# First stage of a layer kernel: order of root, exponentials and softmax weights, order in the last group, and earlier loads of the first patches

## The chip, the cores and the metric

One core of one Trainium2 chip runs the kernel. The metric is device time in microseconds, from one launch to its end. Clock figures are the granted TensorE clock in the profile, as a share of 2.4 GHz.

## The reference

Two images of 256 channels and 96x96 pixels pass one layer: a convolutional part whose nine filter taps per pixel are themselves computed and put through a softmax, and a mixture of experts (two of eight). Cut to what matters here:

```python
def _branch(x, w, d):
    f = lax.conv_general_dilated(x, w, (1, 1), [(d, d), (d, d)], rhs_dilation=(d, d), ...)   # 9 taps per pixel
    f = jax.nn.softmax(f.reshape(N, g, K, H * W), axis=2)
    patches = jnp.stack([xp[:, :, i * d:i * d + H, j * d:j * d + W] for i in range(3) for j in range(3)], axis=2)
    return jnp.einsum('ngrkp,ngkp->ngrp', patches, f)

outs = [x]                                   # x is the layer-normed input here
for w, d in zip((w_a, w_b, w_c, w_d), (1, 4, 8, 12)):
    outs.append(_branch(x, w, d))
y = conv1x1(concatenate(outs), w_proj) + b_proj
x = x + relu(group_norm(y))
x = x + moe(layer_norm(x))                   # router, top 2 of 8 experts, gelu, gated sum
```

## The kernel before

The program runs in stages that all engines leave and enter together (`leave`, `enter`). Each image has a first stage (layer norm, the tap products and the softmax weights) and a second one (the patches are multiplied by their weights and projected); then come the router, the experts and the sum. The change lies in the first stage and at the start of the second.

**First stage.** `GROUPS` = 24 steps `k`, each for `R` = 4 rows of the image. Every engine runs its own written-out list of instructions, in order, and they meet by semaphores. In step `k`:

- TensorE: `channels(k)` turns the normalised rows `xn` back into channels (`ps_ch`); `late_products(k-1)` makes taps 2 and 3 and the two own products of the group before; `tap_products(k, 0)`; `tokens(k+2)` transposes the input of the group after next (L831); `tap_products(k, 1)`. All products go to the two banks of `ps_a` in turn: product `n` waits until product `n-2` has been kept (`wait_free`; the order stands in the list `units`).
- ScalarE: `xc_hi` (L1276), `normalise(k+1, (0, 1))` (`xn`, L1232, needs `nmr`), then copies the late products out (`g_rows` L1241, `y_acc` L1249), `normalise(k+1, (2, 3))`, `keep_products(k, 0)`, in some steps `exponentials`, then `deviation(k+2)` (square root, `std`, L1225) and `keep_products(k, 1)`.
- VectorE: `xc_lo` (L1620), the high half of `rows_st` (L1624), in some steps `lower` (logits less their maximum, L1589 to L1594), `statistics(k+2)` (L1568, L1571), the low half of `rows_st` (L1630), `factors(k+2)` (`rstd`, `nmr`, L1576, L1578), in some steps `weights` (L1602 to L1615).
- GpSimd adds the tap products of the group to the running sums `taps` (L2141).
- SP loads `x_in` and stores `rows_st` to `rows_scratch` in DRAM.

Three groups give a batch of 12 rows; there are 8. Batch `b` is summed up (`logits`, 16 matmuls, L875) in step 3b+7, exponentiated and weighed in that same step, and its filters are turned (`turn_filters`, 2x6 transposes, L885) in step 3b+8. Batches 6 and 7 come behind the last group: their logits wait until GpSimd has added group 23 (`taps_added`). `f_pow` holds one batch's exponentials, `f_low` two batches' logits, later weights; `f16` holds one batch in half precision, and `weights(b)` waits for the turned filters of batch b-1 before it writes it.

**Second stage.** 64 steps. The first 16 are strips, each with 8 loads of patches (112 KB each) from `rows_scratch`: 6 are issued by SP (L677), 2 by GpSimd (L2183), into a ring of three buffers `patches`. The first buffer lies where `x_in` and part of `xn` lie in the first stage. TensorE computes `band(0, 0)`, `band(0, 1)`, `band(1, 0)` (L929), then the branches `ps_o` (L992), which need the patches, and the projections `ps_y`.

## Time and profile before

| | us |
|---|---|
| timed runs, median (lowest to highest) | 2487.01 (2482.56 to 2492.95) |
| profiled execution | 2486.36 |
| its span | 2484.5 |
| first stage, image 0 and image 1 | 21 to 304, 704 to 975 |
| second stage, image 0 and image 1 | 304 to 704, 975 to 1460 |
| mean granted TensorE clock | 0.876 |

| engine | busy us | share of the span |
|---|---|---|
| TensorE | 1950.0 | 78% |
| VectorE | 1626.7 | 65% |
| ScalarE | 1274.9 | 51% |
| GpSimd | 1058.6 | 43% |

The shares are means over stages with different limits, so they say little of one stage. To read the first stage, take the chain of waits: the path of work back from the last instruction, each piece with its start and its length. Then take the same microseconds engine by engine: an entry in square brackets at the end of a line is the idle time in front of the instruction and who ended it. A line that groups several instructions (x8) shows the first start and the time from there to the end of the last. PE is TensorE, DVE VectorE, ACT ScalarE, POOL GpSimd.

### The profile page before, as it was taken

To read this page: it belongs to the slowest core of one execution; us is meant where nothing else is said; L and a number is where in the kernel's file an instruction comes from. 1 tells how busy PE (TensorE), PEld (TensorE's weight loads), DVE (VectorE), ACT (ScalarE), POOL (GpSimd) and SP (SyncE) were. 2 spreads that over 40 slices of the span, in tenths; PEclk is the share of its full clock that TensorE was granted. 3 is DMA by queue.
4 is the path that set the end of the run, shared out by engine and by line. 5 is a ranking of instruction groups with operands and counts; after the bars stand their busy time and mean duration, and the time that the engine had idled before them with its cause. 6 is when DMAs were issued, how large, how long until landed. Compare 5 with 4: busy or idle time off the path is not lost.

```text
span 2484.5 us, 60548 instructions
## 1 busy us (share of the span) xinstructions
PE 1950.0 (78%) x20124; PEld 1843.4 (74%) x20125; DVE 1626.7 (65%) x4385; ACT 1274.9 (51%) x2717; POOL 1058.6 (43%) x1444
## 2 busy tenths in 40 slices
PE   4788699999968886999999928723999999993322
PEld 4677599999957775999999927723999999992222
DVE  3465465656555654777887848852788899894653
ACT  4566343333336663556666626512777777771211
POOL 2454412323225543146566614775555555551000
PEclk9999799999989997999999966556999999995555
DMA  5222155566632222677898787743666444446897
GB/s 135 82 77 77 50 177 149 139 173 169 167 107 83 77 64 86 194 208 241 254 269 263 232 277 250 249 162 128 197 207 192 155 159 162 153 157 212 294 302 252
DMA packets 334948, 433.66 MB, mean 175 GB/s; under 512 B 87469, under 2 KB 260141, under 8 KB 333805
## 3 DMA queue, kind: packets, MB, share of 16 engines
q1 hardware_dynamic: 260945, 294.85, 40.3%
q0 software_dynamic: 41024, 97.10, 11.1%
q10 hardware_dynamic: 32784, 39.07, 4.7%
q8 instruction: 128, 2.10, 0.4%
q14 instruction: 67, 0.55, 0.1%
HBM read 277.12 MB, written 159.94 MB: 176 GB/s over the span
## 4 chain that ended last, share of the span: by engine, by line
PE 47%; DMA 16%; DVE 12%; issue 9%; POOL 6%; ACT 6%; SPq 2%; DVEq 2%; POOLq 0%; ACTq 0%
PE ps_y L418 15%; PE ps L418 9%; DMA expert_out<-e_out,dest 6%; PE ps_a L418 6%; PE ps_o L992 6%; POOL expert_in L2204 5%; PE ps_b L929 4%; DMA o_acc<-res_scratch 3%; DMA o_y<-expert_out 3%; DVE stats L1568 2%; PE ps_x L1140 1%; PE ps_tok L831 1%; PE ps_a L875 1%; DVE rows_st L1630 1%; DVE cat_lo L1663 1%
## 5 line engine op out<-in xcount | busy, mean ns | idle before, releaser
L418 PE MATMUL ps_y<-cat_hi,wp 128*128 128x288 f32 x2048 | 473.7, 307 | 1.9 <-DVE cat_lo L1663 1.9
L2227 POOL DMA_INDIRECT expert_out<-e_out,dest x304 | 306.8, 1009 | 233.2 <-DMA expert_out<-e_out,dest 94.4
L2183 POOL DMA_DIRECT2D patches<-rows_scratch x352 | 196.8, 601 | 468.2 <-PE ps_o L979 262.4
L2141 POOL TENSOR_TENSOR taps<-taps,g_rows 96x108 f32<-96x108 f32 (+3 forms) x440 | 236.9, 566 | 271.5 <-ACT g_rows L1241 267.7
L418 PEld LDWEIGHTS ps_y<-cat_hi,wp 128*128 128x128 f32 x2048 | 346.4, 190 | 2.1 <-issue 1.1
L418 PE MATMUL ps_y<-cat_lo,wp 128*128 128x288 f32 x1024 | 303.8, 297 | 0.0
L1309 ACT ACTIVATE bands<-ps_b 112x288 f16<-112x288 f32 (+4 forms) x256 | 105.3, 411 | 342.9 <-PE ps_b L929 333.0
L1663 DVE SCALAR_TENSOR_TENSOR cat_lo<-ps_o,cat_hi 128x288 fp32r<-128x288 f32 (+1 forms) x576 | 227.3, 419 | 63.9 <-ACT cat_hi L1315 59.5
L1315 ACT ACTIVATE cat_hi<-ps_o 128x288 fp32r<-128x288 f32 (+1 forms) x576 | 212.9, 384 | 65.1 <-PE ps_o L979 30.6
L418 PE MATMUL ps<-e_hi,w_now 128*128 128x256 f32 x1216 | 242.6, 282 | 0.6 <-issue 0.2
L1655 DVE SCALAR_TENSOR_TENSOR bands<-ps_b,bands 112x288 f16<-112x288 f32 (+4 forms) x256 | 116.6, 455 | 191.4 <-ACT bands L1309 188.6
L418 PE MATMUL ps<-w,h_hi 128*128 x1216 | 234.4, 291 | 3.6 <-DVE h_lo L2043 3.6
L992 PE MATMUL ps_o<-bands,patches 112*128 112x72 f16 (+2 forms) x4608 | 193.1, 199 | 24.7 <-DVE cat_lo L1663 14.0
L418 PE MATMUL ps_a<-wg,xc_hi 128*96 128x324 f32 x768 | 187.0, 329 | 29.0 <-ACT g_rows L1241 19.1
L1194 PE MATMUL ps_t<-ident,o_sum 128*128 128x128 f32 x288 | 73.8, 429 | 163.1 <-DVE o_sum L2099 163.1
L2204 POOL DMA_INDIRECT expert_in<-c_ln,pos x144 | 150.5, 1045 | 117.3 <-DVE pos L1899 70.5
L418 PEld LDWEIGHTS ps<-e_hi,w_now 128*128 128x128 f32 x1216 | 197.6, 189 | 3.0 <-issue 2.1
L418 PEld LDWEIGHTS ps_y<-cat_lo,wp 128*128 128x128 f32 x1024 | 195.6, 191 | 0.0
L992 PEld LDWEIGHTS ps_o<-bands,patches 112*128 112x128 f16 (+2 forms) x4608 | 172.0, 101 | 31.6 <-issue 30.4
L1485 ACT ACTIVATE e_act<-ps,b_now 128x256 f32<-128x256 f32 x304 | 127.9, 472 | 121.3 <-PE ps L418 115.7
L1194 PEld LDWEIGHTS ps_t<-ident,o_sum 128*128 128x128 f32 x288 | 54.8, 221 | 181.9 <-issue 172.0
L418 PEld LDWEIGHTS ps<-w,h_hi 128*128 128x128 f32 x1216 | 185.5, 189 | 4.6 <-issue 4.4
(241 smaller groups left out, 4939.1 us busy)
## 6 DMA issues: line engine op xcount, KB each, us to landing
e_x<-expert_in SPq DMA_DIRECT2D x152, 260.0 KB
o_y<-expert_out SPq DMA_DIRECT2D x48, 768.0 KB, 5.3
patches<-rows_scratch SPq DMA_DIRECT2D x160, 192.0 KB
patches<-rows_scratch SPq DMA_DIRECT2D x256, 108.0 KB
patches<-rows_scratch SPq DMA_DIRECT2D x192, 112.0 KB
x_in<-in_x SPq DMA_DIRECT2D x48, 384.0 KB, 3.2
rows_scratch<-rows_st SPq DMA_DIRECT2D x48, 384.0 KB, 3.0
y_scratch<-y_acc SPq DMA_DIRECT2D x48, 384.0 KB
```

The costliest lines, as they stand in the source:

```text
L418: mm = eng.matmul(out, lhs[p], rhs[q], start=start and n == 0, stop=stop and n == 2)
L992: mm = pe.matmul(out, ring[:, (2 * p + z) * C + c * 128:(2 * p + z) * C + (c + 1) * 128], band_of[:, q, p * 72:(p + 1) * 72], start=k == 0 ...
L1194: mm = pe.transpose(ps_t[:, u, c, k * 128:(k + 1) * 128], o_sum[:, u, k, c * 128:(c + 1) * 128], ident[:])
L1309: act.activation(bands[0:k, s % 2, 0, first:first + n], ps_b[0:k, 0:n], ACT.Relu).then_inc(band_hi_done, 1)
L1315: act.activation(cat_pixels(cat_hi[:, s % 2, c], s, j), out_pixels(ps_o[:, n % 2], s), ACT.Copy, scale=UNSCALE).then_inc(cat_hi_done, 1)
L1485: last = act.activation(e_act[:, u, f], ps_1[:, u, f], ACT.Gelu, bias=b1_now[:, u, f:f + 1])
L1655: dve.scalar_tensor_tensor(out=bands[0:k, s % 2, 1, first:first + n], in0=ps_b[0:k, 0:n], scalar=0.0, in1=bands[0:k, s % 2, 0, first:first ...
L1663: dve.scalar_tensor_tensor(out=cat_pixels(cat_lo[:, s % 2, c], s, j), in0=out_pixels(ps_o[:, n % 2], s), scalar=UNSCALE, in1=cat_pixels(ca ...
L2141: last = pool.tensor_tensor(here, here, g_rows[:, u, first:end, i, b:b + nb].rearrange("p r b k -> p r (b k)"), ALU.add)
L2183: pool.dma_start(patch_target(s, n), patch_source(m, s, n)).then_inc(patch_pooled[s % RING], 16)
L2204: pool.indirect_dma_start(out=xs_dram, out_offset=bass.IndirectOffsetOnAxis(ap=at, axis=0), in_=c_ln[:, v, k // TT, k % TT], in_offset=Non ...
L2227: pool.indirect_dma_start(out=ys_dram, out_offset=bass.IndirectOffsetOnAxis(ap=at, axis=0), in_=e_out[:, u, j], in_offset=None).then_inc(e ...
```

## The change

- **Square root**: `deviation(k+2)` moves behind `keep_products(k, 1)` on ScalarE.
- **Exponentials**: both of a pair of batches run in the step of the odd batch (steps 10, 16, 22), in place in `f_low`; `f_pow` goes, and the wait for `f_dve` with it.
- **Weights** (VectorE): batch b (even) one step behind its pair's exponentials, b+1 two steps behind; they stand between `statistics(k+2)` and the low half of `rows_st`. The filters are turned one step after that, so the second one's in the step in which the next pair's first logits come. Batch 4 is weighed in step 23, batch 5 behind the steps.
- **Last group**: taps 2 and 3 first, then the own products with the turned filters of batch 4 between them, the turned filters of batch 5, then the logits of 6 and 7 as before.
- **First patches**: the 8 loads of strip 0 are issued at the end of the first stage, by SP behind its last store and by GpSimd behind its last addition, once `x_in` and `xn` are no longer read and the first rows are stored (`free_first_patches`).

```diff
+        def weighed_in(k):
+
+            b = summed_in(k - 1)
+            if b is not None and b % 2 == 1:
+                return b - 1
+            b = summed_in(k - 2)
+            return b if b is not None and b % 2 == 1 else None
+
         def turned_in(k):
 
-            return (k - 8) // 3 if k >= 8 and (k - 8) % 3 == 0 else None
+            return weighed_in(k - 1)
...
-            late_products(GROUPS - 1)
+            units += [("tap", m_, GROUPS - 1, 2), ("tap", m_, GROUPS - 1, 3)]
+            units += [("own", m_, GROUPS - 1, 0), ("turned", m_, BATCHES - 4, 0), ("own", m_, GROUPS - 1, 1), ("turned", m_, BATCHES - 4, 1)]
+            units += [("turned", m_, BATCHES - 3, 0), ("turned", m_, BATCHES - 3, 1)]
...
+        def free_first_patches(eng, m):
+
+            eng.wait_ge(tok_ready, (m + 1) * GROUPS)
+            eng.wait_ge(ch_ready, (m + 1) * GROUPS)
+            eng.wait_ge(rows_done, (m + 1) * GROUPS)
+            for u in range(2):
+                eng.wait_ge(rows_stored[u], 16 * (m * (GROUPS // 2) + 2))
+            eng.wait_ge(pads_zeroed, 16 * 4 * IMAGES)
...
+                free_first_patches(sp, m)
+                for n in range(loads(0)):
+                    if not second_queue(0, n):
+                        sp.dma_start(patch_target(0, n), patch_source(m, 0, n)).then_inc(patch_loaded[0], 16)
...
-                    after(act, f_dve, 3 * (m * BATCHES + b))
-                    act.activation(f_pow[:], f_low[:, b % 2], ACT.Exp).then_inc(f_exp, 1)
+                    act.activation(f_low[:, b % 2], f_low[:, b % 2], ACT.Exp).then_inc(f_exp, 1)
...
                     keep_products(k, 0)
-                    if summed_in(k) is not None:
-                        exponentials(summed_in(k))
+                    keep_products(k, 1)
                     if k + 2 < GROUPS:
                         deviation(k + 2)
-                    keep_products(k, 1)
+                    if summed_in(k) is not None and summed_in(k) % 2 == 1:
+                        exponentials(summed_in(k) - 1)
+                        exponentials(summed_in(k))
...
                     if k + 2 < GROUPS:
                         statistics(k + 2)
+                    if weighed_in(k) is not None:
+                        weights(weighed_in(k))
                     dve.wait_ge(rows_hi_done, N + k + 1)
                     dve.scalar_tensor_tensor(out=rows_st[:, u, :, 1], in0=xn[:, u], scalar=SCALE, in1=rows_st[:, u, :, 0],
                                              op0=ALU.mult, op1=ALU.subtract).then_inc(rows_done, 1)
                     if k + 2 < GROUPS:
                         factors(k + 2)
-                    if summed_in(k) is not None:
-                        weights(summed_in(k))
...
+                weights(BATCHES - 3)
...
+                free_first_patches(pool, m)
+                for n in range(loads(0)):
+                    if second_queue(0, n):
+                        pool.dma_start(patch_target(0, n), patch_source(m, 0, n)).then_inc(patch_pooled[0], 16)
```

On TensorE and ScalarE the last group is written in the same order as in `units`; `weights` reads and writes `f_low` where it read `f_pow`; the second stage's loops skip the loads of strip 0.

## Rows read from the trace of the kernel before

**Rows 1.** Stretch of the first stage: busy us (instructions) by engine, granted clock, DMA share, GB/s

```profile
801.00:832.00 31.00, 25.36 (x186) 23.08 (x185) 18.71 (x47) 20.34 (x41) 16.09 (x32) 1.00 0.26 78
```

**Rows 2.** Chain of waits, longest pieces: start us, us, what; three without a batch, one with

```profile
760.70 3.03 PE ps_a L418 x18
769.55 3.03 PE ps_a L418 x18
...
800.65 3.02 PE ps_a L418 x18
```

**Rows 3.** Chain of waits inside a step, then behind the logits of a batch

```profile
806.45 1.17 DVE rows_st L1630
...
807.74 0.17 DVE nmr L1578
...
807.93 0.02 ACT xn L1232
...
809.33 1.74 PE ps_a L875 x16
811.07 2.03 PE ps_a L418 x12
```

**Rows 4.** Instructions of VectorE in order of time: start us, us, engine, line, operation

```profile
804.58 1.42 DVE L1568 BATCH_NORM_STATS2 stats<-ps_tok 96x6 f32<-96x256 f32 x4 [3.90 <-PE ps_tok L831]
...
818.74 0.59 DVE L1602 TENSOR_REDUCE fred<-f_pow 96x48 f32<-96x432 f32 x1
...
820.90 0.60 DVE L1615 TENSOR_TENSOR f<-f_low,f 96x432 f16<-96x432 f32 x1
```

**Rows 5.** Instructions of TensorE: the token transposes of three steps in a row

```profile
803.50 1.03 PE L831 MATMUL ps_tok<-ident,x_in 128*96 128x128 f32 x8
...
813.81 1.03 PE L831 MATMUL ps_tok<-ident,x_in 128*96 128x128 f32 x8
...
825.81 1.03 PE L831 MATMUL ps_tok<-ident,x_in 128*96 128x128 f32 x8
```

**Rows 6.** Instructions of ScalarE in the step of an exponential

```profile
814.95 1.28 ACT L1256 ACT_TABLE_LOAD   x1
816.25 0.56 ACT L1256 ACTIVATE f_pow<-f_low 96x432 f32<-96x432 f32 x1
...
819.34 1.01 ACT L1232 ACTIVATE xn<-ps_tok,nmr,rstd 96x256 f32<-96x256 f32 x2
```

**Rows 7.** Instructions of ScalarE at the start of the first stage

```profile
22.77 1.28 ACT L1225 ACT_TABLE_LOAD   x1
27.50 0.30 ACT L1225 ACTIVATE std<-mv,eps 96x4 f32<-96x4 f32 x1 [3.44 <-DVE mv L1571]
```

**Rows 8.** Chain of waits at the end of image 1's first stage

```profile
946.25 3.23 PE ps_a L418 x12
...
960.10 6.01 PE ps_a L875 x32
```

**Rows 9.** Instructions of GpSimd: seven additions, beside `rows_st` and alone

```profile
938.41 4.61 POOL L2141 TENSOR_TENSOR taps<-taps,g_rows 96x432 f32<-96x432 f32 x7 [4.41 <-ACT g_rows L1241]
...
948.63 3.38 POOL L2141 TENSOR_TENSOR taps<-taps,g_rows 96x432 f32<-96x432 f32 x7 [3.65 <-ACT g_rows L1241]
```

**Rows 10.** TensorE at the start of the second stage, image 0, then image 1

```profile
310.90 1.60 PE L992 MATMUL ps_o<-bands,patches 112*128 112x72 f16 x24 [4.06 <-DMA patches<-rows_scratch]
...
315.00 1.60 PE L992 MATMUL ps_o<-bands,patches 112*128 112x72 f16 x24
...
987.17 1.60 PE L992 MATMUL ps_o<-bands,patches 112*128 112x72 f16 x24 [5.63 <-DMA patches<-rows_scratch]
```

**Rows 11.** Busy times, columns as in rows 1, of stretches behind waits of TensorE

```profile
242.70:245.80 3.10, 3.10 (x12) 3.10 (x12) 0.76 (x2) 1.08 (x2) 0.74 (x1) 0.52 0.00 0
...
956.00:960.00 4.00, 0.19 (x2) 0.00 (x0) 0.00 (x0) 0.58 (x1) 3.88 (x9) 0.89 0.00 0
960.00:966.00 6.00, 5.90 (x32) 5.79 (x32) 1.81 (x3) 0.56 (x1) 0.00 (x0) 0.51 0.00 0
```

More of the change, by code:

```diff
@@ L252, in build @@
             f_low = sbuf(r1, "f_low", [W, 2, R2 * FCOL])
-            f_pow = sbuf(r1, "f_pow", [W, R2 * FCOL])
             f16 = sbuf(r1, "f16", [W, R2, 2, FCOL], F16)
@@ L702, in _ @@
                         kept += 1
-                    load_patches(s)
+                    if s:
+                        load_patches(s)
                     behind = s - UNITS1 - 18
@@ L914, in _ @@
                     step(k)
-                late_products(GROUPS - 1)
+                tap_products(GROUPS - 1, 2)
+                tap_products(GROUPS - 1, 3)
+                for o in range(CC):
+                    own_products(GROUPS - 1, o)
+                    turn_filters(BATCHES - 4, o)
+                for o in range(CC):
+                    turn_filters(BATCHES - 3, o)
                 logits(BATCHES - 2)
@@ L1294, in _ @@
                     step(k)
-                late_products(GROUPS - 1)
+                keep_products(GROUPS - 1, 2)
+                keep_products(GROUPS - 1, 3)
+                for o in range(CC):
+                    keep_own(GROUPS - 1, o)
+                    keep_filters(BATCHES - 4, o)
+                for o in range(CC):
+                    keep_filters(BATCHES - 3, o)
                 exponentials(BATCHES - 2)
@@ L1601, in weights @@
                     dve.wait_ge(f_exp, done + 1)
-                    dve.tensor_reduce(fred[:, 1], nine(f_pow[:]), AX.X, ALU.add).then_inc(f_dve, 1)
+                    dve.tensor_reduce(fred[:, 1], nine(f_low[:, b % 2]), AX.X, ALU.add).then_inc(f_dve, 1)
                     dve.wait_ge(f_dve, base + 1)
@@ L1605, in weights @@
                     dve.wait_ge(f_dve, base + 2)
-                    dve.scalar_tensor_tensor(out=nine(f_low[:, b % 2]), in0=nine(f_pow[:]), scalar=SCALE,
+                    dve.scalar_tensor_tensor(out=nine(f_low[:, b % 2]), in0=nine(f_low[:, b % 2]), scalar=SCALE,
                                              in1=fred[:, 3].unsqueeze(2).broadcast_to([W, R2 * NB, TAPS]),
@@ L2177, in _ @@
                 thirds = 0
-                for s in range(STEPS):
+                for s in range(1, STEPS):
                     shared = [n for n in range(loads(s)) if second_queue(s, n)]
```

## The prediction

> **What bounds the kernel now.** I read the busy times by stage first: the first stage runs twice, 21 to 304 us and 704 to 975 us, and in 31 us of it TensorE is busy for 25.36, VectorE for 18.71, ScalarE for 20.34 [rows 1]. No engine is full, so a loop of waits sets the pace. Of the second stage the change touches only the start. The profiled execution took 2486.36 us (span 2484.5); the median of the three timed runs is 2487.01, so I sum against 2486.4 and take the result as the median too.
>
> Next I read the chain of waits through the first stage. Every step without a batch gives one 18-matmul piece, 8.85 us after the one before [rows 2]. Inside a step the chain is a loop [rows 3]: tokens transposed on TensorE, statistics (1.42 [rows 4]), `mv`, the low half of `rows_st` (1.17), `rstd` and `nmr`, all on VectorE; then ScalarE's `xn` at 807.93, 0.02 behind the end of `nmr`; then `g_rows` of tap 2, which frees the PSUM bank for the next 3 us of matmuls, behind which the next tokens come. The reader is to see that whatever stands on VectorE between `mv` and `nmr` lengthens the step by its full duration, and that what stands behind `nmr` has room until the next statistics (VectorE waits 3.9 us there [rows 4]).
>
> A batch makes three steps take 31.1 us (769.55 to 800.65 [rows 2]) instead of 3x8.85=26.55: 4.5 us per batch. By the starts of the token transposes (803.50, 813.81, 825.81 [rows 5]) the step with the logits takes 10.31 (+1.46, the logits' 1.74 less slack) and the one with the turned filters 12.00 (+3.15). The latter holds a load of tables, the exponential, a load back and the late `std` [rows 6], which put `xn` at 819.34, 5.53 us behind the tokens where a plain step has 4.43 (+1.1); a wait of the transposes for the weights (to 821.66, about +0.85); and waits for `y_acc` (about +1.1).
>
> **The change part by part, per image.** I time six steps (two batches), all from the start of the tokens.
>
> *Square root behind the copies.* `g_rows` of tap 1 is ready before `mv` and no longer waits behind `std`. The matmuls that it frees had lost 0.18 us, in a place where `nmr` ends later: nothing gained in a plain step. ScalarE's slack before `xn` grows from 0.1 to about 0.4 us.
>
> *Exponentials in pairs* (steps 10, 16, 22). Behind `std` (ends at +3.28): one load 1.28, two exponentials at a pitch of 0.47, then `xc_hi`, 0.70 further `xn`: at 6.24 against 4.43 [rows 5, 6]. That is +1.8 in steps 11 and 17, against 1.1 per batch before. The load back to the root is issued when `g_rows` is done, not when `mv` is there: at the stage's start it ran 22.77 to 24.05 and `std` came only at 27.50 [rows 7]. So I cost it at nothing: it lies in ScalarE's idle time before `mv`, and would cost up to 1.3 if it could not.
>
> *The weights in front of `rows_st`.* Batches 0 to 3 are weighed in steps 11, 12, 17, 18, between `mv` and `nmr`. The five instructions take 2.70 us (818.74 to 821.50 [rows 4]), where they used to stand behind `nmr` (the first of them starts as `nmr` ends). By the loop above this is +2.7 each, uncovered: `xn` is queued behind `nmr`, `g_rows` behind `xn`, and all TensorE's late products behind that. In return the turned filters (steps 12, 13, 18, 19) find their input ready. Step 12 and 18: 2.7, plus 0.5 (tap 3 now waits for `y_acc`, not `g_rows`), plus 0.8 (tap 0 waits for the second `y_acc`, as before): +4.0. Step 13 and 19 hold logits and turned filters together: 2.7 + 1.5 (logits) + 1.0 (tap 3 must wait until VectorE has read the logits, 0.60 and two hand-overs) + 0.8 = +6.0.
>
> Up to step 22 the new extras are 4x1.46 + 2x1.8 + 2x4.0 + 2x6.0 = 29.4 us; the old ones 5x4.5 + 1.46 = 24.0. **Loop: +5.4 us** (bounds +2, if half a weighing finds cover, and +8).
>
> *The last group.* In step 22 ScalarE's `xc_hi` comes 0.5 later, but nothing of batch 5 is turned in step 23: that takes away the wait to 945.59 and the half-rate piece of 3.23 us for 12 matmuls [rows 8]. Following the queues, tap 3 of group 23 ends at 950.2 instead of 954.9 (1.0 of it because it stands before `own`), GpSimd's last addition ends near 955.0 instead of 959.95, and the logits start at 955.9, since `weights(5)` must wait for the turned filters of batch 4 and logits 6 for the turned ones of batch 5. The additions of taps now run beside the weights: seven of them took 3.38 us alone and 4.61 beside `rows_st` [rows 9], so 0 to 2 us is lost. The logits took 6.01 us [rows 8] at half rate; behind transposes and `own` products they would run as the 1.74 of [rows 3], and the second batch's chain follows the first with no gap: another 2.3. 959.95 to 973.4 shrinks so. **Last group: -6.4, less 0.4 for the additions: -6.0** (bounds -3 and -7.2). Exp 7 loses its wait for `f_dve`, off the chain.
>
> *First strip's patches.* TensorE waited 4.06 us (image 0) and 5.63 (image 1) for them [rows 10]. Now SP issues its six behind the last store, near 950, when it has nothing else (some 5 us of issuing, landing near 960, stage end near 969); GpSimd's two (0.6 us each) lie behind its last addition and in front of its leave, under 13 us of VectorE work. What is late next: strip 1. Its DMAs take the issue slots that strip 0 had and land where strip 0 did (310.8 and 987.1), while strip 0's matmuls last 4.05 us (310.90 to 315.00 [rows 10]). So image 0 gains 4.05 whole and image 1, capped by strip 1 (landing 987, where its matmuls used to start at 991.2, four behind strip 0's), about 4.3. **Patches: -4.2** (bounds -3 and -5).
>
> *The clock.* Granted 1.00 (2.4 GHz) in such a stretch of the loop [rows 1]. After the idle 956.2 to 960.1 TensorE ran 6 us at 0.51 (1.2 GHz), and even waits of 1.5 us, twice in a step, were followed by 3.1 us at 0.52 once per image [rows 11]. The change makes waits of about 4.2 us in steps 12, 13, 18, 19 (from the end of `own` 0, some 4.4 behind the tokens, to 8.6) and 3.3 us in steps 11 and 17. I take it that the clock falls after nearly all of them. At half rate 12 matmuls took 3.23 against 2.03, the logits 3.0 against 1.74 [rows 3, 8]. I charge 1.0 for steps 11 and 17, 1.6 for 12 and 18, 2.1 for 13 and 19: 9.4, less 1.4 for the old fall that is replaced: **+8.0** (bounds 0 and +17). The upper bound is the half rate lasting from the wait to the tokens in all six.
>
> The Trainium skill, "TensorE: Matmul & The Clock Gate", under "HAM oscillation", says that a kernel which waits between blocks of matmuls can start each of them cold. It speaks against this change, and the rows above say the same.
>
> Sum per image: 5.4 - 6.0 - 4.2 + 8.0 = +3.2; two images +6.4 (2492.8). Because the half rate may also shorten the waits behind it, I say 2492.
>
> One rule would give another number. The Trainium skill, "ScalarE: Activation LUTs", "What ACT_TABLE_LOAD costs", puts a switch of tables at about 2.66 us, a drain of 1.38 behind the load counted in. Here the next instruction starts 0.01 us behind the 1.28 [rows 6], so no drain shows. By the page each image's 6 removed loads would free 16 us of ScalarE instead of 7.7; the measured duration decides.
>
> **The rivals.**
>
> 1. *The same chain, but the clock stays high.* For it: waits of 1.5 us mostly left it at 1.00 in steps like 801 to 832 [rows 1]. Against it: the one longer idle time of this stage was followed by 0.51 [rows 11]. Sum: 2x(5.4 - 6.0 - 4.2) = -9.6: 2476.8.
>
> 2. *The weights are hidden after all*, so the change does what its parts suggest: the loop falls by 4x2.7 to -5.4 and no long waits arise: 2x(-5.4 - 6.0 - 4.2) = -31: 2455. Against it: `xn` starts 0.02 us behind `nmr` [rows 3], no slack.
>
> 3. *Slower: the half rate rules the loop.* Place: tap 3, `own` 1, tap 0 and the tokens behind each long wait. At half rate throughout, that stretch takes 8.2 instead of 4.9 us (from 3.23 against 2.03 for its main part). 3.3 in each of six steps is 19.8, less 1.4: per image 5.4 - 6.0 - 4.2 + 18.4 = +13.6, together +27: 2513. It decides from a clock cost of about 11 us per image on. For it: the 6 us at 0.51 behind a 3.9 us idle time [rows 11].
>
> 4. *The patches don't come early*, or strip 1 takes the wait over: 2x4.2 back: 2501.
>
> **How the numbers follow.** Forecast 2492 (its own range 2481 to 2502): 0.50. Rival 1: 0.17. Rival 2: 0.07. Rival 3: 0.20. Rival 4: 0.06. With the bounds of the terms, 8 in 10 lie between 2472 and 2507. 0.5%, about what a measurement of this kernel can tell from no change, is 12.4 us. Faster than 2474.6: rival 2 and part of rival 1, 0.15. Slower than 2499.4: rivals 3 and 4 and a little of the forecast, 0.28. Same: 0.57.
>
> **What would show it.** After: token starts of steps 12 and 13 about 12.8 and 14.8 us behind those before, plus the clock; `rows_st` behind five weight instructions; TensorE idle for some 4 us before the turned filters, and a granted clock near 0.5 behind it; 12 loads of tables fewer; the last logits about as long as 2x1.74; no wait for patches at strip 0, and a short one or none at strip 1. If steps 12 and 13 last under 11 us, the loop is misread. If the clock stays at 1.00, rival 1 holds.

## The result and the profile after

The changed kernel takes 2510.23 us (2501.28 to 2513.96) where the kernel before takes 2487.55 (2482.56 to 2494.75): a ratio of **1.0083, 95% interval 1.0058 to 1.0107**. It is slower by 0.8%. The forecast was 2492 with a range up to 2507, so the result lies 18 us above the forecast and 3 us outside the range.

The profiled execution took 2510.71 us, its span is 2508.9, TensorE's mean granted clock 0.867 where it was 0.876. The page of the changed kernel, engines first, then the granted clock over the span in 40 slices:

```profile
PE 1959.9 (78%) x20124; PEld 1866.3 (74%) x20125; DVE 1627.2 (65%) x4385; ACT 1264.3 (50%) x2705; POOL 1059.6 (42%) x1444
...
PEclk9989999999989888999999965556999999995555
```

TensorE executes the same 20124 instructions and is busy for 10 us longer, at a lower granted clock. ScalarE has 12 instructions fewer, the 12 loads of tables, and is busy for 10.6 us less; what this is worth in time no run isolates.

**Where the time went.** From the first to the last token transposes (steps 0 to 21) the changed kernel takes 251.3 and 240.7 us in images 0 and 1, where the kernel before takes 235.1 and 224.3: +16.2 and +16.4. From the last transposes to the second stage's first matmul it takes 44.25 and 43.55 instead of 46.4: -2.2 and -2.9. The second stages, up to the next stage's first work, are shorter by 6.0 and 7.7 us. At the first load behind them (`c_x`) the changed kernel stands 13.6 us behind. From there to the end, in code that the change doesn't touch, it takes another 10.7 us longer (1041.1 against 1030.3); more on that below.

The starts of steps 9 to 14 of image 1, by their token transposes, instructions of TensorE in the changed kernel (start us, length us; the counterpart of [rows 5]):

```profile
799.76 1.03 PE L854 MATMUL ps_tok<-ident,x_in 128*96 128x128 f32 x8
...
808.56 1.03 PE L854 MATMUL ps_tok<-ident,x_in 128*96 128x128 f32 x8
...
818.88 1.04 PE L854 MATMUL ps_tok<-ident,x_in 128*96 128x128 f32 x8
...
831.80 1.47 PE L854 MATMUL ps_tok<-ident,x_in 128*96 128x128 f32 x8
...
846.99 1.03 PE L854 MATMUL ps_tok<-ident,x_in 128*96 128x128 f32 x8
...
864.11 1.03 PE L854 MATMUL ps_tok<-ident,x_in 128*96 128x128 f32 x8
```

A plain step still lasts 8.8 us and the one with logits 10.3. Then come 12.9, 15.2 and 17.1 us: steps 11 (behind the exponentials), 12 (weights and turned filters) and 13 (weights, logits and turned filters). In image 0 they last 11.9, 14.4 and 17.5, and steps 17 to 19 in both images 11.9, 14.6 to 14.8 and 17.1 to 17.4. Before, a batch gave 12.0 once and nothing above, but for one step of 13.5 per image.

Inside step 12, VectorE, the counterpart of the weights in [rows 4], now ahead of `rows_st` and `nmr`, which ends 7.5 us behind the tokens (4.4 in a plain step):

```profile
834.80 0.37 DVE L1606 BATCH_NORM_AGGREGATE mv<-stats 96x2 f32<-96x6 f32 x4
835.09 0.57 DVE L1637 TENSOR_REDUCE fred<-f_low 96x48 f32<-96x432 f32 x1
...
837.23 0.60 DVE L1650 TENSOR_TENSOR f<-f_low,f 96x432 f16<-96x432 f32 x1
837.76 1.21 DVE L1667 SCALAR_TENSOR_TENSOR rows_st<-xn,rows_st 96x1024 f16<-96x1024 f32 x1
...
839.09 0.16 DVE L1613 SCALAR_TENSOR_TENSOR nmr<-mv,rstd 96x4 f32<-96x4 f32 x1
```

ScalarE and TensorE behind it (in square brackets the idle time before the instruction and who ended it):

```profile
839.29 1.01 ACT L1261 ACTIVATE xn<-ps_tok,nmr,rstd 96x256 f32<-96x256 f32 x2 [2.31 <-DVE nmr L1613]
```

```profile
840.68 0.69 PE L908 MATMUL ps_ft<-ident,f 96*72 96x96 f16 x6 [3.95 <-ACT g_rows L1270]
...
855.43 2.18 PE L898 MATMUL ps_a<-taps,shift 96*96 96x108 f32 x16 [3.93 <-ACT g_rows L1270]
```

The reader is to see the chain of the prediction: `mv`, five weight instructions, `rows_st`, `nmr`, `xn`, and TensorE waits 3.9 us for the copy that is queued behind. Then the granted clock of the stretches around it (columns as in rows 1):

```profile
790.00:819.00 29.00, 24.67 (x181) 23.52 (x180) 16.06 (x42) 17.29 (x38) 17.71 (x33) 1.00 0.29 83
819.00:832.00 13.00, 9.84 (x54) 9.42 (x53) 5.09 (x13) 8.36 (x17) 7.36 (x17) 0.76 0.21 61
...
841.50:847.00 5.50, 5.22 (x25) 4.90 (x25) 0.00 (x0) 2.89 (x6) 3.18 (x7) 0.56 0.01 4
857.00:864.00 7.00, 6.41 (x34) 5.96 (x33) 1.81 (x3) 2.82 (x6) 3.02 (x7) 0.54 0.00 0
864.00:873.00 9.00, 7.66 (x56) 7.30 (x55) 4.62 (x13) 5.27 (x12) 2.82 (x6) 1.00 0.29 89
```

Behind the two long waits shown TensorE works for 5.5 and 7 us, nearly without a gap, at 0.56 and 0.54, which is the lower level (1.2 GHz) for nearly the whole stretch, and is back at 1.00 when the next plain step runs.

The start of the second stage, image 1, TensorE, against [rows 10]:

```profile
1002.78 1.63 PE L1021 MATMUL ps_o<-bands,patches 112*128 112x72 f16 x24
...
1007.27 0.94 PE L1021 MATMUL ps_o<-bands,patches 112*128 112x72 f16 x24 [0.42 <-DMA patches<-rows_scratch]
```

No wait for patches at strip 0, and 0.42 us at strip 1.

### The profile page after: what moved, and what is told of

Read it like the earlier page. It is cut to its first block, busy times and chain, and to the rows that moved or that the text cites. A ratio compares the mean times of both kernels' runs of the same rounds, so it can differ in the third digit from the quotient of the medians.

```text
span 2508.9 us, 60533 instructions
## 1 busy us (share of the span) xinstructions
PE 1959.9 (78%) x20124; PEld 1866.3 (74%) x20125; DVE 1627.2 (65%) x4385; ACT 1264.3 (50%) x2705; POOL 1059.6 (42%) x1444
## 4 chain that ended last, share of the span: by engine, by line
PE 48%; DMA 17%; DVE 13%; issue 8%; POOL 6%; ACT 5%; SPq 2%; DVEq 1%; POOLq 0%; ACTq 0%
PE ps_y L417 14%; PE ps L417 9%; DMA expert_out<-e_out,dest 6%; PE ps_a L417 6%; PE ps_o L1021 5%; POOL expert_in L2244 4%; PE ps_b L958 4%; DMA o_acc<-res_scratch 3%; DMA o_y<-expert_out 3%; DVE stats L1603 2%; DVE rows_st L1667 2%; PE ps_tok L854 2%; DMA expert_in<-c_ln,pos 2%; PE ps_x L1169 1%; PE ps_a L898 1%
## 5 line engine op out<-in xcount | busy, mean ns | idle before, releaser
L417 PE MATMUL ps_a<-wg,xc_hi 128*96 128x324 f32 x768 | 194.3, 340 | 64.0 <-ACT g_rows L1270 55.8
L1021 PE MATMUL ps_o<-bands,patches 112*128 112x72 f16 (+2 forms) x4608 | 191.7, 199 | 16.3 <-DVE cat_lo L1699 14.5
L1603 DVE BATCH_NORM_STATS2 stats<-ps_tok 96x6 f32<-96x256 f32 x192 | 68.1, 414 | 185.3 <-PE ps_tok L854 185.3
```

Source lines behind the costliest of these rows:

```text
L417: mm = eng.matmul(out, lhs[p], rhs[q], start=start and n == 0, stop=stop and n == 2)
L1021: mm = pe.matmul(out, ring[:, (2 * p + z) * C + c * 128:(2 * p + z) * C + (c + 1) * 128], band_of[:, q, p * 72:(p + 1) * 72], start=k == 0 ...
L1603: dve.bn_stats(stats[0:W, k % 2, r], ps_tok[0:W, k % 2, r])
```

## The experiments

Experiments 5 to 8 ran on a second chip and 9 to 11 on a third; on these the kernel before takes 2677 and 2678 us. Image 1's second stage is longer there (614 us in run 5, 471 in the first profile of the same kernel), and so is what follows it. Each ratio is to the kernel before on the same chip. The kernel before was profiled on neither, so where its steps and stages are named they are those of its one profile; the changed kernel's first stages take the same on both chips that have it, but for 3 us in image 1.

**1. The weights put back behind `nmr`,** all else as changed:

```diff
                         statistics(k + 2)
-                    if weighed_in(k) is not None:
-                        weights(weighed_in(k))
                     dve.wait_ge(rows_hi_done, N + k + 1)
...
                         factors(k + 2)
+                    if weighed_in(k) is not None:
+                        weights(weighed_in(k))
```

> The changed kernel with one move: the weights of a batch stand behind the factors (rstd, nmr) of the same step, not in front of rows_st. Theory A (the 2.7 us of weights stand in the loop between mv and nmr, and the waits that they make drop TensorE's clock): the steps that took 12.9, 15.2 and 17.1 us (steps 11, 12, 13 of image 1) take about 12, 10.1 and 12.1, some 10 us less per pair of batches, 40 us less in all: about 2468, 0.992 of before. Theory B (the pairing of the exponentials, with two of them and a load of tables between std and xn, is what costs): steps 12 and 13 stay above 14 us and the kernel stays at about 1.008.

Measured: 2481.14 us against 2493.82, ratio **0.9947 (0.9925 to 0.9969)**. This one move turns the slower kernel into a faster one than before, though by less than expected (0.992). Its loop takes 239.4 and 230.4 us, 11.8 and 10.3 less than the changed kernel's. Steps 11 to 13 of image 1 still last 12.0, 11.5 and 15.1 us (10.1 and 12.1 had been expected for the last two), so its loop is 4 to 6 us longer than before, where the prediction's rival 2 had it 5.4 shorter. The waits of TensorE over 155 us of its loop in image 0 (line that waited, who it waited for: us in total, times, the longest) show why:

```profile
PE ps_a L417 <- ACT g_rows L1270: 13.5, 7, 3.2
PE ps_a L898 <- ACT g_rows L1270: 6.5, 5, 1.4
PE ps_ft L908 <- DVE f L1650: 5.8, 2, 3.0
PE ps_a L417 <- DVE f_low L1624: 2.8, 2, 1.4
```

Two of its steps in image 0, one of the kind of step 12 and one of the kind of step 13 (columns as in rows 1), in which the clock stayed up:

```profile
152.62:164.09 11.47, 8.18 (x66) 7.60 (x64) 7.25 (x18) 8.29 (x17) 4.94 (x12) 1.00 0.22 69
230.58:243.58 13.00, 9.86 (x83) 9.24 (x80) 8.89 (x21) 6.43 (x14) 3.31 (x8) 1.00 0.23 62
```

At a full clock these steps thus take 11.5 and 13.0 us, where the changed kernel's take 12.9 and 14.8 (run 6 below). So of the 2.7 us of a weighing only 1.4 and 1.8 came back, 6.5 us per image; the rest of the 11.8 and 10.3 is mostly clock. With the weights behind `nmr` the turned filters wait for them (up to 3.0 us), the pair of exponentials leaves a wait of 3.2, and step 13 waits for logits read late. The granted clock over this stretch is 0.96, between the 0.99 of the kernel before and the 0.91 of the changed one.

**2. Only the weights moved ahead,** in the kernel before:

```diff
                         statistics(k + 2)
+                    if summed_in(k) is not None:
+                        weights(summed_in(k))
...
                         factors(k + 2)
-                    if summed_in(k) is not None:
-                        weights(summed_in(k))
```

> The kernel before with one move: the weights of a batch in front of rows_st, in the same step as before. Nothing else of the change. Theory A: nmr is 1.7 us later than before in each batch step, the turned filters no longer wait (0.85 back), and the wait of about 4 us before the late products drops TensorE's clock (some 1.7 more): +2.5 per batch, five batches per image in the loop, 25 us in all, about 1.010 of before. Theory B (the place of the weights does not matter, they are hidden): 1.000, steps with turned filters stay at 12.0 us.

Measured: 2518.95 us, ratio **1.0101 (1.0075 to 1.0127)**, +25 us. The step with the turned filters lasts 14.6 to 15.0 us instead of 12.0, some 2.7 more. That this is the length of the five instructions is chance: `nmr` ends 7.2 us behind the tokens instead of 5.0, so 2.2 later (in that step the square root had held it up by some 0.6 already; 1.7 had been expected), the turned filters' wait of 1.5 for the weights is gone, and the granted clock of nine of the ten steps is 0.77 where it was 1.00 in eight of ten.

**3. Only the first patches' early loads,** in the kernel before:

```diff
+                free_first_patches(sp, m)
+                for n in range(loads(0)):
+                    if not second_queue(0, n):
+                        sp.dma_start(patch_target(0, n), patch_source(m, 0, n)).then_inc(patch_loaded[0], 16)
...
-                    load_patches(s)
+                    if s:
+                        load_patches(s)
```

> The kernel before with the loads of the first strip's patches issued at the end of the first stage, nothing else. Theory A: no wait for patches in front of strip 0; image 0 gains its whole wait of 4.06 us, image 1 gains until strip 1's patches land, 4.3 to 5: 8 to 9 us in all, 0.9965. Theory C (the second stages of the changed kernel were 6.0 and 7.7 us shorter, so more than the wait is gained): 13 to 14 us, 0.9945. Theory D (the earlier transfers get in the way of the first stage's end): no gain, 1.000.

Measured: 2480.82 us, ratio **0.9955 (0.9939 to 0.9970)**. The second stages take 396.2 and 471.3 us instead of 402.1 and 478.5: -5.9 and -7.1 per image, where the prediction had -4.2. TensorE in image 0 and image 1 of this kernel:

```profile
306.87 1.63 PE L1006 MATMUL ps_o<-bands,patches 112*128 112x72 f16 x24
...
980.00 1.60 PE L1006 MATMUL ps_o<-bands,patches 112*128 112x72 f16 x24 [1.41 <-DMA patches<-rows_scratch]
```

No wait at strip 0, one of 1.41 us at strip 1 in image 1, as against 4.06 and 5.63 [rows 10].

**4. The clock kept up, first size.** In the long waits TensorE multiplies the identity by itself into a part of `ps_tok` that the next tokens overwrite; nothing reads the result:

```diff
                         own_products(k, o)
+                        if o == 0:
+                            for _ in range(FILL.get(k + 1, 0)):
+                                pe.matmul(ps_tok[:, (k + 1) % 2, 0, 0:128], ident[:], ident[:], start=True, stop=True, skip_group_check=True)
...
+                FILL = {11: 28, 12: 36, 13: 36, 17: 28, 18: 36, 19: 36}
```

> The changed kernel with 28 or 36 matmuls of 128x128 without use, written to a PSUM bank that is free at that time, behind the first own product in steps 11, 12, 13, 17, 18, 19, in the waits in front of the late products. Theory A with the clock: the granted clock stays at 1.00, steps 11, 12, 13 take 10.6, 12.8 and 14.8 us instead of 12.9, 15.2 and 17.1; some 12 us per image are won back, 25 in all: about 2485, 0.999 of before. Theory A without the clock (the chain of VectorE alone sets the steps): nothing changes, 1.008. If the filling matmuls delay the late products, a step is longer than that.

Measured: 2529.28 us, ratio **1.0145 (1.0119 to 1.0172)**. The clock stayed at 1.00 in the loop, but a filler takes 0.22 us, about twice what I had allowed, and so they overran the waits by 2.9 to 3.9 us: steps 11 to 13 lasted 13.5, 16.6 and 18.7. It doesn't tell the theories apart by its time; it only gave the size for the next run of the kind.

**5. The changed kernel again,** unchanged, beside runs 6 to 8:

> The changed kernel once more, beside the other kernels of this call: a second profile of it, to see which part of its +24.4 us in the first one comes back. Theory A: the first stages are again 16 us longer up to the last tokens and the second stages 6 and 7 to 8 us shorter, while the time from the first c_x load to the end, which the change does not touch, lies anywhere in 1030 to 1041 us as in the six profiles so far; 1.008 of before. Rival: the stages behind are really longer by some 10 us because of the change, so that they take 1041 us again.

Measured: 2692.54 us against 2676.80, ratio **1.0075 (1.0047 to 1.0104)**. Loops of 251.2 and 237.7 us and last groups of 44.3 and 44.5 come again. What follows the first `c_x` takes 1078.2 us on this chip, which can't be set against the 1041 of the other; see the sum below.

**6. The clock kept up, shorter:** as 4, with

```diff
+                FILL = {11: 13, 12: 17, 13: 17, 17: 13, 18: 17, 19: 17}
```

> As e4_clock_kept_up, but with 13 or 17 filling matmuls, since one took 0.22 us there and 36 of them overran the wait of 4.2 us by 3.7. Theory A with the clock: granted clock 1.00, steps 11, 12, 13 take 10.6, 12.8 and 14.8 us (the steps of e4, 13.5, 16.6 and 18.7, less 2.9, 3.7 and 3.8 of overrun) instead of 12.9, 15.2 and 17.1; some 11 us per image are won back, about 0.999 of before. Theory A without the clock: no change, 1.008.

Measured: 2663.92 us, ratio **0.9948 (0.9931 to 0.9965)**. The starts of steps 11 to 14 of image 1:

```profile
807.50 1.03 PE L854 MATMUL ps_tok<-ident,x_in 128*96 128x128 f32 x8
...
818.04 1.04 PE L854 MATMUL ps_tok<-ident,x_in 128*96 128x128 f32 x8
...
830.90 1.04 PE L854 MATMUL ps_tok<-ident,x_in 128*96 128x128 f32 x8
...
845.73 1.03 PE L854 MATMUL ps_tok<-ident,x_in 128*96 128x128 f32 x8
```

10.5, 12.9 and 14.8 us for steps 11 to 13: these are the times that follow from the prediction's terms at a full clock (10.6, 12.8 and 14.8: a plain step and +1.8, +4.0, +6.0). And the clock over image 0's loop, changed kernel again (5) and with fillers (6):

```profile
100.00:255.00 155.00, 119.95 (x813) 113.85 (x812) 80.91 (x204) 84.42 (x176) 69.60 (x138) 0.91 0.23 67
```

```profile
100.00:255.00 155.00, 139.13 (x1068) 133.56 (x1067) 85.70 (x218) 90.78 (x189) 74.38 (x147) 1.00 0.25 72
```

The loops take 241.0 and 228.0 us, 10.2 and 9.6 less than in run 5: **that is what the half rate cost per image**, with the same chain of waits. What is left over the kernel before, whose loop is counted without the 1.5 us of its own fall, is the chain: 228.0 less 222.8, +5.2, in image 1, and 241.0 less 233.6 in image 0, +5.9 once the 1.5 us of step 6 are taken out (see experiment 9). The forecast was +5.4. So 188 matmuls that compute nothing, 94 per image, make the changed kernel 1.3% faster, faster than before. By the two loops it should be 20 us faster; the timed runs differ by 28.6, and 8 us of that lie in the untouched later stages of the two profiled executions.

The Trainium skill, "TensorE: Matmul & The Clock Gate", under "HAM oscillation", says that a kernel that waits between its blocks of matmuls can start every one of them cold; these two runs agree, with 1.00 against 0.91 over the stretch and 10 us per image.

**7. The last group without its weights.** Batches 4 and 5 are weighed for one row of twelve only; the rest of their weights is left out:

```diff
+                    short = b in (BATCHES - 4, BATCHES - 3)
+                    some, n_rows = (NB, 1) if short else (R2 * NB, R2)
...
-                    dve.tensor_copy(f16[:, :, 0], filters).then_inc(f_hi_done, 1)
+                    dve.tensor_copy(f16[:, 0:n_rows, 0], filters[:, 0:n_rows]).then_inc(f_hi_done, 1)
```

> The changed kernel, where the weights of batches 4 and 5 are computed for one row of twelve only (the other rows of these batches get no weights of their own; the output is not the reference's). All waits and semaphores stay. Theory E (VectorE's weights and GpSimd's additions slow each other in the last group): the additions of groups 22 and 23 take 4.7 and 4.2 us instead of 6.1 and 5.2, the last logits start 2.5 us earlier, and with a shorter wait in front of them they may run at the full rate, another 1.6: the first stage is 2.5 to 4 us shorter per image behind its last tokens. Rival F (the additions are late because the copies of g_rows are): no change of the tail.

Measured in one execution (2682.18 us): from the last tokens to the second stage 41.65 and 40.5 us, where the changed kernel takes 44.28 and 44.48 on this chip: -2.6 and -4.0. GpSimd's additions of groups 22 and 23 and TensorE's logits in image 1, first in the changed kernel, then in this one:

```profile
970.75 5.27 POOL L2177 TENSOR_TENSOR taps<-taps,g_rows 96x432 f32<-96x432 f32 x7 [2.10 <-ACT g_rows L1270]
...
976.37 5.81 POOL L2177 TENSOR_TENSOR taps<-taps,g_rows 96x108 f32<-96x108 f32 x11
```

```profile
982.32 5.10 PE L898 MATMUL ps_a<-taps,shift 96*96 96x108 f32 x32 [1.51 <-POOL taps L2177]
```

```profile
964.47 4.39 POOL L2179 TENSOR_TENSOR taps<-taps,g_rows 96x432 f32<-96x432 f32 x7 [2.12 <-ACT g_rows L1270]
...
969.23 5.21 POOL L2179 TENSOR_TENSOR taps<-taps,g_rows 96x108 f32<-96x108 f32 x11
```

```profile
974.58 3.22 PE L898 MATMUL ps_a<-taps,shift 96*96 96x108 f32 x32 [1.28 <-POOL taps L2179]
```

Two things cost the last group its gain: the additions lose 1.5 us beside the weights (5.27 and 5.81 against 4.39 and 5.21), and the logits run at half rate for most of their time (5.10 us, or 5.98 in run 5) where they take 3.22 at full clock, 1.9 to 2.8 us. Without the weights image 1's last group is 5.9 us shorter than before, image 0's, where the logits take 4.85 us, 4.8.

**8. Another order.** In the kernel before: the early patches, taps 2 and 3 first in the last group, and each batch's filters turned one step later, two behind its logits. Exponentials, weights and root stay where they were:

```diff
-            return (k - 8) // 3 if k >= 8 and (k - 8) % 3 == 0 else None
+            return (k - 9) // 3 if k >= 9 and (k - 9) % 3 == 0 else None
...
-                late_products(GROUPS - 1)
+                tap_products(GROUPS - 1, 2)
+                tap_products(GROUPS - 1, 3)
+                for o in range(CC):
+                    own_products(GROUPS - 1, o)
+                    turn_filters(BATCHES - 3, o)
```

> The kernel before, with each batch's exponentials and weights where they were (behind nmr), its filters turned two steps behind the logits instead of one, those of batch 5 between the own products of the last group behind taps 2 and 3, and the first strip's patches loaded early. Theory A (weights behind nmr are free, and the wait of the transposes for them is what they cost): 0.85 us less per batch, 4 us per image in the loop; the last group about 5 us shorter, since nothing waits for the weights of batch 5 and no weights stand beside the additions; second stages 6 and 7 us shorter as with the patches alone: 28 us in all, about 0.989. Rival: turning a step later only moves the wait, and the gain stays that of the patches, 0.9955.

Measured: 2655.27 us, ratio **0.9924 (0.9902 to 0.9946)**. A batch takes steps of 9.9, 10.2 and 10.2 us, 30.3 instead of 31.1, and none of 12.0; two steps per image last 11.2 to 11.3. The gain lies between the whole (0.989) and the patches alone (0.9955): the last group is 3.8 us shorter, not 5, with its logits at half rate still (6.00 us).

**9. Only the root behind the copies,** in the kernel before:

```diff
+                    keep_products(k, 1)
                     if k + 2 < GROUPS:
                         deviation(k + 2)
-                    keep_products(k, 1)
```

> The kernel before with the square root behind the copies (deviation(k+2) behind keep_products(k, 1)), nothing else. By the loop (nmr sets xn) the plain steps stay at 8.7 to 8.9 us. Theory G: the own products run earlier, so in image 0, where a store holds everything up from 60 to 82 us, TensorE has nothing left to run behind the hold-up until xn and g_rows are there, and its clock rises later: step 6 takes 19.0 instead of 17.5 us, as in all kernels with this move so far. In the steps with an exponential std stands behind the load of tables as before. Sum +1 to +2 us, 1.000 to 1.001. Rival: step 6 is longer because of the weights or the pairing, then it takes 17.5 here.

Measured: 2687.24 us, ratio **1.0037 (1.0020 to 1.0054)**: slower, by some 10 us where 1 to 2 were expected. The waits of TensorE over the same 155 us as in 1, in the kernel before and in this one:

```profile
PE ps_a L418 <- ACT g_rows L1241: 13.9, 20, 1.5
PE ps_ft L885 <- DVE f L1615: 7.7, 5, 1.5
PE ps_a L875 <- ACT g_rows L1241: 4.5, 5, 0.9
PE ps_a L418 <- ACT y_acc L1249: 2.5, 5, 0.5
```

```profile
PE ps_ft L885 <- DVE f L1615: 17.3, 5, 3.5
PE ps_a L875 <- ACT g_rows L1241: 6.8, 5, 1.4
PE ps_a L418 <- ACT g_rows L1241: 5.4, 4, 1.3
PE ps_a L418 <- ACT y_acc L1249: 1.4, 4, 0.5
```

The own products no longer wait for a copy behind the root, so they run earlier, and then TensorE stands in front of the turned filters for as long as it stood in two places before: 28.6 us of waiting have become 30.9 (`nmr` ends 0.3 us later in those steps), but 1.5 and 1.5 have become 3.5 at a stretch. And behind such a stretch the clock is lower. The wait of step 9 in image 1, and the 6 us behind it:

```profile
802.14 0.42 PE L885 MATMUL ps_ft<-ident,f 96*72 96x96 f16 x6 [3.47 <-DVE f L1615]
```

```profile
802.00:808.00 6.00, 5.58 (x36) 5.19 (x37) 1.46 (x2) 3.44 (x7) 3.71 (x8) 0.72 0.01 3
```

The step with the turned filters lasts 13.4 to 14.7 us instead of 12.0, and the clock fell in all ten of them, where it fell in two of ten before. Step 6 of image 0, where the stores hold the loop up, lasts 18.2 instead of 17.5; 19.0 had been expected, which is what the changed kernel has. Up to that step this kernel and the changed one differ from the kernel before by this move alone, and over all profiled executions it takes 18.2 to 19.7 us with the move and 17.4 to 17.9 without.

**10. Only taps 2 and 3 first in the last group,** in the kernel before:

```diff
-                late_products(GROUPS - 1)
+                tap_products(GROUPS - 1, 2)
+                tap_products(GROUPS - 1, 3)
+                for o in range(CC):
+                    own_products(GROUPS - 1, o)
```

> The kernel before, where the last group's taps 2 and 3 stand in front of its two own products; nothing else. The additions of group 23 start 1.0 us earlier, TensorE's wait in front of the last logits is 1.0 shorter in the middle and filled by own products, 3.9 - 2.0 = 1.9 us of it left; the logits start 1.0 us earlier. If the clock falls all the same they take 6.0 us (first stage 1.0 shorter per image); if it stays up, 3.5 (3.5 shorter per image). I expect 1 to 2.5 us per image, 2 to 5 in all: 0.998 to 0.999.

Measured: 2671.12 us, ratio **0.9968 (0.9946 to 0.9989)**. The last group takes 42.7 and 42.8 us instead of 46.4, -3.7, where 1 to 2.5 were expected: more than in the changed kernel, which adds the turned filters of two batches and the weights to it. Its loops, which the edit doesn't touch, hold four steps of 13.4 to 14.2 us, where the profile of the kernel before has two of 13.5.

**11. The kernel of 8 again,** beside 9 and 10:

> The same kernel as e8_turned_a_step_later, for a narrower interval and on a chip where the second stage of image 1 may be faster: the step intervals of 9.9, 10.2, 10.2 per batch and a last group some 3.9 us shorter come again, 0.9895 of before if the whole gain (2.3 loop, 3.9 last group, 6 to 7 second stage, per image) shows, 0.9925 if it is as in e8.

Measured: 2646.71 us, ratio **0.9875 (0.9849 to 0.9902)**. The waits of TensorE over 150 us of its loop:

```profile
PE ps_a L418 <- ACT g_rows L1261: 12.9, 20, 1.5
PE ps_ft L901 <- ACT g_rows L1261: 4.1, 5, 0.9
```

The turned filters no longer wait for `f`, and no wait is longer than 1.5 us. Image 1's loop takes 219.2 us (222.0 in run 8) where the kernel before has 224.3. This kernel beats both. The two ratios of this same kernel, on two chips, only touch with their intervals, so its gain is known to no better than 0.8 to 1.3%.

## Why the prediction was right and wrong

**Right: the chain, and the weights' place in it.** At a full clock steps 11 to 13 are 10.5, 12.9 and 14.8 us (run 6), as the terms give them, and `nmr` ends 7.0 us behind the tokens in steps 12 and 13, for 4.3 to 4.5 with the weights behind it (run 1): 2.6 to 2.7 later, "+2.7 each, uncovered". The loop's +5.4 measured +5.2 and +5.9. That run 1 gave back 11.8 and 10.3 us per image, close to 4x2.7 = 10.8, is chance: at a full clock it gave back 1.4 and 1.8 per step, since the turned filters then wait for the weights, and the rest is mostly clock. The load back to the root cost nothing by itself, as said: 1.28 us at 834.69, while ScalarE had nothing else, and `std` ended 2.8 us ahead of `nmr`. Rival 2 is gone: with the weights out of the chain the loop at a full clock would be some 1 us shorter than before (+5.4 less 6.5, an estimate from runs 1 and 6), not 5.4.

**Right: the clock, within its bounds.** 9.4 us of half rate were charged to the six steps, and run 5 against run 6 has 10.2 and 9.6; less the 1.4 to 1.5 of the kernel before, that is +8.7 and +8.2 for +8.0. It fell behind all twelve waits in the first profile and behind eleven of twelve in run 5, as taken. Run 5's loops come to 5.9 + 8.7 + 1.5 (step 6) = +16.1 in image 0 and 5.2 + 8.2 = +13.4 in image 1, for +13.4 forecast. The profiled execution had +16.2 and +16.4: in its image 1 steps 11 and 12 took 12.9 and 15.2 us where run 5 has 10.6 and 14.4, so the length of the half rate differs by 3 us between executions. Rival 1 is gone: the clock does not stay high by itself.

**Failed: "Square root behind the copies: nothing gained in a plain step."** True of plain steps, and there the working stopped. In a step with turned filters the earlier own products shift waiting time behind them, and the stretches join (run 9, +0.37%). In the changed kernel the batches are laid out otherwise, so that run 9's figure is not its share; what can be named there is step 6 of image 0, +1.5 us, for which the prediction had no term. Rival 2's price (2455) was out of reach for the clock as well: in run 1 the loop was 4.4 and 6.1 us longer than before, by waits for `f` and `f_low` and by a clock of 0.96.

**Failed: the last group.** This is the step that cost the forecast most: -6.0 worked out, -2.2 and -2.9 measured, 7 us in the sum of both images. The -6.4 in it were 4.2 for an earlier start of the logits and 2.3 for a full clock behind it. The logits started only 2.0 us earlier (28.8 us behind the last tokens, for 30.8 before), because GpSimd's last addition ended late: "0 to 2 us is lost" beside the weights was charged at 0.4 and was 1.5 (run 7), and even without the weights the additions end 1.5 us later than worked out, which stays open. And "behind transposes and `own` products they would run as the 1.74 of [rows 3]" did not hold: waits of 1.61 and 1.51 us with 1.15 us of transposes between them stand in front of the logits, which start at the half rate again and give back 0.9 us in image 1 and 0.1 in image 0 instead of 2.3:

```profile
977.00:982.00 5.00, 2.21 (x23) 1.86 (x21) 1.32 (x2) 2.30 (x4) 4.84 (x10) 0.75 0.52 153
982.00:988.00 6.00, 5.10 (x32) 4.94 (x32) 2.35 (x4) 0.56 (x1) 1.33 (x3) 0.64 0.15 43
```

The prediction did have the first of these waits ("since `weights(5)` must wait"), but not the clock behind them. Without the weights (run 7) the last group gained 5.9 and 4.8 us, near the forecast, so it is the weights left in this group that cost most of it.

**Mis-sized the other way: the patches.** -4.2 forecast, -5.9 and -7.1 in run 3. The wait for strip 0 went, as said, and strip 1 waits 0.42 to 1.41 us in image 1, the short one foreseen. The rest comes in the following bands: in image 0 the gain is 4.3 us at strip 0 and 5.1 at the sixth band, and TensorE, without the wait, reaches the full clock some 7 us behind the first band instead of 14. Rival 4 is gone.

**The sum.** By stages the profile has 2x(16.3 - 2.5) less 6.0 and 7.7 us of the second stages, +13.6 at the first `c_x`, where the forecast had +6.4: +7 from the last groups, +6 from the loops (step 6, and in image 1 of this execution a longer half rate), -5 from the patches. The ratios of the timed runs give +20 on both chips, so some 7 us come from elsewhere. In the untouched rest the profiled execution took 1041.1 us against 1030.3, while runs 1 to 4, with the same code there, took 1036.3, 1037.7, 1032.6 and 1035.5. So executions of it lie up to 10 us apart and the two compared are the lowest and the highest; how much of the 7 us between +13.6 and +20 is such scatter (or scatter of the loops and the early stages), and how much the change does to the later stages, **stays open**: on the other chip run 5 took 1078.2 us for it and run 6 1070.1, so the changed kernel has the longer rest in that pair too; but run 10, the kernel before with one edit to the last group, took 1079.6 on the third chip, for 1071.2 of run 9. And run 1 is out by as much the other way: -6 us at the first `c_x`, -13 by its timed runs.

Rival 3's number is the one that came in, by luck: its time (2513) is within 3 us of the measured one, with a different composition. It had the half rate throughout all six steps (+18.4 per image, net); measured are 8.2 to 8.7, so its mechanism did not come in at that size, and the last group and the part left open fill the gap. What decided was thus not the term with the widest bounds but one with narrow bounds (-3 to -7.2) that the measurement left. Rival 3 had a chance of 0.20 and stood at 2513, outside the range of 2472 to 2507: the range ought to have reached it.

## What to carry to other kernels

In a loop of waits, work put between the producer's last result and the operation that the others wait for delays all of them by its length (`nmr` 2.6 to 2.7 us later), and moving it behind that operation decided the sign here (1.0083 against 0.9947). But a place behind it is not free where something else waits for the result: of 2.7 us only 1.4 and 1.8 came back at a full clock. Before an edit that moves work earlier on the matmul engine, look at what waiting times it joins: about the same idle time cost the clock in ten steps of ten when it came in one piece, and in two of ten when it came in two. The better cure was not to move the exponentials or weights at all but to use their result one step later, so that no wait is left for it (0.9924 and 0.9875, with the early patches and the order of the last group, which alone gave 0.9955 and 0.9968).

## What the runs showed of the hardware

- **Clock.** Waits of 3.5 to 3.95 us are followed by 5 to 7 us at 0.54 to 0.72. Those of 3.2 us behind the exponentials were followed by a fall in seven of eight cases (the two traces of the changed kernel). Two of 1.5 us in a step were not in eight of ten (kernel before). Filler matmuls in the wait hold it at 1.00. Why single steps of 13.5 us appear in the kernels without long waits, now in one batch and now in another, stays open.
- **Filler.** An f32 matmul of 128x128 into 128 columns takes 0.22 us in its turn at full clock, twice the 0.10 to 0.13 us that the token transposes take (8 in 1.03 us [rows 5]); by those I had sized run 4.
- **VectorE beside GpSimd.** In the last group a scalar_tensor_tensor of 96x432 took twice its usual time while GpSimd added, and seven additions 5.27 us, for 3.38 alone [rows 9]. VectorE in the changed kernel, the same instruction beside the additions and, but for its last 0.2 us, without them:

```profile
971.12 1.22 DVE L1641 SCALAR_TENSOR_TENSOR f_low<-f_low,fred 96x432 f32<-96x432 f32 x1
...
975.99 0.60 DVE L1641 SCALAR_TENSOR_TENSOR f_low<-f_low,fred 96x432 f32<-96x432 f32 x1
```

The Trainium skill, "GPSIMD Engine Reference", "Key points", says that GpSimd shares its SBUF interfaces with VectorE and meets instructions with two SBUF inputs there; this one has two, and the rows agree, with 0.62 us on it. On the additions beside the weights it is 0.9 us (5.27 against 4.39 in run 7); the rest of the 1.9 stands beside `rows_st`, a scalar_tensor_tensor with two inputs as well.
